# Cross attention: a batch's output projection in two parts of four pairs, with eight places for outputs and four for halves

## What is computed

```python
qh = (q @ wq.T).reshape(B, Sq, N_HEADS, HEAD_DIM).transpose(0, 2, 1, 3)
kh = (k @ wk.T).reshape(B, Sk, N_HEADS, HEAD_DIM).transpose(0, 2, 1, 3)
vh = (v @ wv.T).reshape(B, Sk, N_HEADS, HEAD_DIM).transpose(0, 2, 1, 3)
scores = jnp.einsum('bhqd,bhkd->bhqk', qh, kh) / jnp.sqrt(jnp.float32(HEAD_DIM))
attn = jax.nn.softmax(scores, axis=-1)
ctx = jnp.einsum('bhqk,bhkd->bhqd', attn, vh)
ctx = ctx.transpose(0, 2, 1, 3).reshape(B, Sq, N_HEADS * HEAD_DIM)
return ctx @ wo.T
```

## Time and profile before

| | us |
|---|---|
| median of 3 executions | 3653.69 |
| lowest and highest | 3648.0, 3655.38 |
| span of the profiled execution, first to last instruction | 3648.2 |
| cross attention, first row maximum to the last low half (rows below) | 1853.5 to 3440.3 |
| its 32 steps that open a batch, batches 1, 2, 3 | 205.2, 204.7, 206.4 |
| its 32 steps that close a batch, batches 0, 1, 2 | 197.1, 198.7, 197.3 |

### The profile page before, as it was taken

How to read it: one execution, slowest core, us unless ns; L and a number is a source line. 1 busy time by engine, 2 the same in 40 slices (tenths; PEclk the granted TensorE clock), 3 DMA queues, 4 the chain that set the end, 5 groups by cost and what they waited for, 6 DMA issues and landing times. The chain is left out here.

```text
span 3648.2 us, 78625 instructions
## 1 busy us (share of the span) xinstructions
PE 3088.9 (85%) x31124; PEld 1836.6 (50%) x31124; DVE 2698.1 (74%) x4017; ACT 2360.0 (65%) x4397; POOL 1058.4 (29%) x1854
## 2 busy tenths in 40 slices
PE   6999999978999755899778888998899879998824
PEld 3747474645665543444345554555455545555411
DVE  4748483867897765444469988889888988889688
ACT  3838373766786534333368887778777887788534
POOL 2232323156446234233212222222222222222122
PEclk9999999989999977999999999999999999999956
DMA  4050505175365376344399999999999999999843
GB/s 151 28 146 29 172 5 146 37 249 149 122 201 165 94 251 208 81 119 127 92 220 190 190 199 199 199 202 186 214 196 200 189 214 194 199 201 184 158 158 124
DMA packets 1309823, 582.40 MB, mean 160 GB/s; under 512 B 1144338, under 2 KB 1230994, under 8 KB 1306900
## 3 DMA queue, kind: packets, MB, share of 16 engines
q1 hardware_dynamic: 1305428, 560.60, 69.3%
q0 software_dynamic: 4032, 16.78, 1.2%
HBM read 183.63 MB, written 109.45 MB: 80 GB/s over the span
## 5 line engine op out<-in xcount | busy, mean ns | idle before, releaser
L2296 DVE SCALAR_TENSOR_TENSOR ca_halves<-ca_probs,ca_inv,ca_halves 128x1024 f16<-128x1024 f32 x512 | 655.5, 1280 | 109.9 <-ACT ca_halves L2222 102.4
L2288 DVE TENSOR_REDUCE ca_neg_max<-banks 128x1 f32<-128x1024 f32 x512 | 623.8, 1219 | 64.1 <-PE banks L2066 62.6
L2222 ACT ACTIVATE ca_halves<-ca_probs,ca_inv 128x1024 f16<-128x1024 f32 x512 | 586.6, 1146 | 102.9 <-DMA ca_pt<-ca_halves 99.1
L2214 ACT ACTIVATE ca_probs<-banks,ca_neg_max 128x1024 f32<-128x1024 f32 x512 | 568.7, 1111 | 72.6 <-DVE ca_neg_max L2288 70.7
L2032 POOL TENSOR_SCALAR ca_inv<-ca_total 128x1 f32<-128x1 f32 x512 | 97.5, 190 | 1197.1 <-ACT ca_probs L2214 1197.1
L2066 PE MATMUL banks<-ca_kt,ca_qt 64*128 64x512 f16 x3072 | 381.3, 382 | 48.8 <-ACT ca_probs L2214 47.1
L2088 PE MATMUL banks<-ca_pt,ca_v 128*64 128x256 f16 x6144 | 388.6, 277 | 0.9 <-DMA ca_pt<-ca_halves 0.8
L2088 PEld LDWEIGHTS banks<-ca_pt,ca_v 128*64 128x64 f16 x6144 | 318.6, 111 | 94.2 <-issue 78.4
L2035 POOL TENSOR_TENSOR ca_inv<-ca_inv,ca_minus_one 128x1 f32<-128x1 f32 x512 | 280.3, 548 | 42.6
L2066 PEld LDWEIGHTS banks<-ca_kt,ca_qt 64*128 64x128 f16 x3072 | 132.6, 95 | 238.8 <-issue 95.0
L2047 PE MATMUL banks<-ca_ct,ca_w 128*128 128x512 f16 x768 | 180.5, 386 | 48.1 <-DMA ca_ct<-ctx_part 23.8
(11 more groups left out here) (306 smaller groups left out, 5738.7 us busy)
## 6 DMA issues: line engine op xcount, KB each, us to landing
ca_w<-ca_w_parts SPq DMA_DIRECT2D x32, 768.0 KB, 5.4
wa_v<-v_rows SPq DMA_DIRECT2D x44, 264.0 KB, 4.5
v_rows<-wa_v_stage SPq DMA_DIRECT2D x32, 264.0 KB, 2.2
wa_x<-in_x SPq DMA_DIRECT2D x32, 256.0 KB, 5.3
wa_ring<-in_x SPq DMA_DIRECT2D x32, 256.0 KB, 3.9
x_after_window_attention<-wa_ring SPq DMA_DIRECT2D x32, 256.0 KB, 3.1
ba_tokens<-wa_tok_turned SPq DMA_DIRECT2D x32, 256.0 KB, 3.6
ba_xt<-ba_tokens SPq DMA_DIRECT2D x32, 256.0 KB, 7.2
```

The costliest lines, as they stand in the source:

```text
L2214: act.activation(probs[:, slot, :], scores(i), ACT.Exp, bias=neg_max[:, slot:slot + 1], accum_out=total[:, slot:slot + 1]).then_inc(exped, 1)
L2222: act.activation(halves[:, slot, 0, :], probs[:, slot, :], ACT.Copy, scale=inv[:, slot:slot + 1]).then_inc(split_hi, 1)
L2288: dve.tensor_reduce(out=neg_max[:, slot:slot + 1], in_=scores(i), axis=X_AXIS, op=ALU.max, negate=True).then_inc(maxed, 1)
L2296: dve.scalar_tensor_tensor(out=halves[:, slot, 1, :], in0=probs[:, slot, :], scalar=inv[:, slot:slot + 1], in1=halves[:, slot, 0, :], op0= ...
```

## The change

The output projection of batches 0, 1 and 2 is made in two parts, as it was in the last batch before. The first part is pairs 0 to 3, in steps 34, 37, 42, 45, 54, 55, 56 and 57 of the *same* batch; DVE adds each result to the residual rows. The second part is pairs 4 to 7, in the old places in the next batch. Each part has 12 matmuls for each tile where there were 24. The last batch keeps its six and two pairs. Steps that now hold a first part are no longer free for a flip, so 12 flips are left of 36, and 24 more units send both halves through the DMA transpose. `ca_ot` goes from 11 places to 8, and ACT waits for the part that last read a place (`released`). `ca_halves` goes from 3 places to 4, so `high_half` of unit i waits for the transpose of unit i-4; `ca_probs` and the score banks keep three.

```diff
-OT_SLOTS = PAIRS + 3
+OT_SLOTS = PAIRS
+HALF_SLOTS = 4
@@
-        halves = sb("ca_halves", [P, SLOTS, 2, S], F16)
+        halves = sb("ca_halves", [P, HALF_SLOTS, 2, S], F16)
@@
+        def first_step(b, t):
+            return BATCH * b + (34, 37, 42, 45, 54, 55, 56, 57)[t]
+
+        def tile_pairs(b):
+            return range(PAIRS // 2, PAIRS) if b + 1 < B else range(EARLY_PAIRS, PAIRS)
+
+        def early_step(b, t):
+            return first_step(b, t) if b + 1 < B else STEPS - 10 + t
+
+        def early_pairs(b):
+            return range(PAIRS // 2) if b + 1 < B else range(EARLY_PAIRS)
+
+        def released(turn, at):
+
+            b, pair = divmod(turn, PAIRS)
+            return 2 * NT * b + (NT if pair >= len(early_pairs(b)) else 0) + 2 * at + 2
@@
-        partly_at = {STEPS - 10 + t: t for t in range(NT)}
+        partly_at = {early_step(b, t): (b, t) for b in range(B) for t in range(NT)}
@@ SP
                             sp.dma_start_transpose(pt[:, step % 4, h, 0:parts * NT, :],
-                                                   halves[:, i % SLOTS, 0:parts, :].rearrange("p q s -> p (q s)")
-                                                   ).then_inc(turned[i % SLOTS], 16)
+                                                   halves[:, i % HALF_SLOTS, 0:parts, :].rearrange("p q s -> p (q s)")
+                                                   ).then_inc(turned[i % HALF_SLOTS], 16)
@@ PE
-                        out_product(b, t, range(PAIRS) if b + 1 < B else range(EARLY_PAIRS, PAIRS)).then_inc(out_projected, 1)
+                        out_product(b, t, tile_pairs(b)).then_inc(out_projected, 1)
                     if step in partly_at:
+                        b, t = partly_at[step]
                         spare_free(step)
                         pe.wait_ge(wo_loaded, 32)
-                        pe.wait_ge(ot_lo, GROUPS * (B - 1) + 4 * EARLY_PAIRS)
-                        out_product(B - 1, partly_at[step], range(EARLY_PAIRS)).then_inc(partly_projected, 1)
+                        pe.wait_ge(ot_lo, GROUPS * b + 4 * len(early_pairs(b)) - 4 + t // 2 + 1)
+                        out_product(b, t, early_pairs(b)).then_inc(out_projected, 1)
@@ ACT
-                    if i >= SLOTS:
-                        act.wait_ge(turned[slot], turned_by(i - SLOTS))
+                    if i >= HALF_SLOTS:
+                        act.wait_ge(turned[i % HALF_SLOTS], turned_by(i - HALF_SLOTS))
@@ ACT
-                        act.wait_ge(out_projected, NT * (last_use // PAIRS) + 2 * (g % 4) + 2)
+                        act.wait_ge(out_projected, released(last_use, g % 4))
```

More of the change, by code:

```diff
@@ L1903, in cross_attention @@
         split_hi, split_lo = sem("ca_split_hi"), sem("ca_split_lo")
-        turned = [sem(f"ca_turned{i}") for i in range(SLOTS)]
+        turned = [sem(f"ca_turned{i}") for i in range(HALF_SLOTS)]
         weighted, ot_hi, ot_lo = sem("ca_weighted"), sem("ca_ot_hi"), sem("ca_ot_lo")
         out_projected = sem("ca_out_projected")
-        partly_projected, partly_added = sem("ca_partly_projected"), sem("ca_partly_added")
+        partly_added = sem("ca_partly_added")
         qscale = 1.0 / (WS * DX ** 0.5)
@@ L1945, in turned_by @@
         def turned_by(i):
-            return 16 * (i // SLOTS + 1)
+            return 16 * (i // HALF_SLOTS + 1)
         def qk_item(turn, i, bank):
@@ L2077, in weigh @@
                             pe.wait_ge(ot_lo, g)
-                        for i in range(4 * g + 1, 4 * g + 4):
-                            pe.wait_ge(turned[i % SLOTS], turned_by(i))
+                        for i in range(4 * g, 4 * g + 4):
+                            pe.wait_ge(turned[i % HALF_SLOTS], turned_by(i))
                         if flips_until(4 * g + 3):
@@ L2122, in flip_low @@
                         last = pe.transpose(bank[:, kb * P:(kb + 1) * P],
-                                            halves[:, i % SLOTS, 1, kb * P:(kb + 1) * P], consts.ident_h[:, :])
+                                            halves[:, i % HALF_SLOTS, 1, kb * P:(kb + 1) * P], consts.ident_h[:, :])
                     last.then_inc(low_flipped, 1)
@@ L2219, in high_half @@
                     act.wait_ge(inverted, i + 1)
-                    if i >= SLOTS:
-                        act.wait_ge(turned[slot], turned_by(i - SLOTS))
-                    act.activation(halves[:, slot, 0, :], probs[:, slot, :], ACT.Copy,
+                    if i >= HALF_SLOTS:
+                        act.wait_ge(turned[i % HALF_SLOTS], turned_by(i - HALF_SLOTS))
+                    act.activation(halves[:, i % HALF_SLOTS, 0, :], probs[:, slot, :], ACT.Copy,
                                    scale=inv[:, slot:slot + 1]).then_inc(split_hi, 1)
@@ L2272, in low_item @@
                         rows = n.residual_rows(dve, b, t)
-                        dve.wait_ge(out_projected, NT * b + t + 1)
-                        if b + 1 == B:
-                            dve.wait_ge(partly_added, t + 1)
+                        dve.wait_ge(out_projected, 2 * NT * b + NT + t + 1)
+                        dve.wait_ge(partly_added, NT * b + t + 1)
                         dve.scalar_tensor_tensor(out=rows, in0=psum[:, SPARE, :], scalar=1 / WS, in1=rows,
@@ L2278, in low_item @@
                     if step in partly_at:
-                        t = partly_at[step]
-                        rows = n.residual_rows(dve, B - 1, t)
-                        dve.wait_ge(partly_projected, t + 1)
+                        b, t = partly_at[step]
+                        rows = n.residual_rows(dve, b, t)
+                        dve.wait_ge(out_projected, 2 * NT * b + t + 1)
                         dve.scalar_tensor_tensor(out=rows, in0=psum[:, SPARE, :], scalar=1 / WS, in1=rows,
@@ L2293, in low_half @@
                     dve.wait_ge(split_hi, i + 1)
-                    if i - SLOTS in flipped_units:
-                        dve.wait_ge(low_flipped, flips_until(i - SLOTS))
-                    dve.scalar_tensor_tensor(out=halves[:, slot, 1, :], in0=probs[:, slot, :],
-                                             scalar=inv[:, slot:slot + 1], in1=halves[:, slot, 0, :],
+                    if i - HALF_SLOTS in flipped_units:
+                        dve.wait_ge(low_flipped, flips_until(i - HALF_SLOTS))
+                    dve.scalar_tensor_tensor(out=halves[:, i % HALF_SLOTS, 1, :], in0=probs[:, slot, :],
+                                             scalar=inv[:, slot:slot + 1], in1=halves[:, i % HALF_SLOTS, 0, :],
                                              op0=ALU.mult, op1=ALU.subtract).then_inc(split_lo, 1)
```

## The result

The changed kernel takes 3632.95 us (median of 4, 3626.99 to 3635.51) beside 3654.53 us of the kernel before in the same comparison: a ratio of 0.9939, 95% interval 0.9926 to 0.9953. It is faster by 21.6 us. The prediction said 3588 us, range 3562 to 3628: the direction was right, the size a third of the forecast, and the time lies outside the range. The profiled execution took 3635.51 us.

A forecast was written before the change was run, and what follows sets the result against it. PE was taken to bind the opening halves of batches 1 to 3, nothing shown the closing ones. Terms -52 - 2 - 9 - 2 = -65 us took the 3648.2 us span to 3583, plus 5.5 gives 3588; range 3562 to 3628.

The forecast's parts named there:

- Tile turns: Opening halves of batches 1 to 3: twelve turns go from 616.3 us to 564, 47.0 each, -52 us.
- a tile step is now a step like the six of the yardstick: Opening halves: a tile step costs what six balanced full steps cost before, 5.82 us, so eight are 46.6 us.
- it is not above ... unless the queue binds: Upper bound of an opening turn: no longer than the present 51.4 us (gain 0) unless the transpose queue binds.
- I take -3 us a batch, near the byte count less one unit: Last ten steps of batches 0 to 2: -3 us each, -9 in all, bounds -9 to +6 a batch.
- The fourth place: Extra place for halves, in batch 0's opening half and the last batch's closing half: -2 us, between 0 and some -10.
- now stall PE: Last ten steps of a batch: flips that hold PE waiting for ACT's copy, 17.9 us in all, would be gone.
- The other closing turns: Closing halves of batches 0 to 2, two turns before the context loads: 47.1 us becomes 46.7, -2 us in all.
- Three places just suffice: Places for halves: a loop of some 7.4 us fits three units' 8.7 us, so waits are short; four give 11.6.
- Rival B: Places for halves were the stage's real loop, so more of the 99.1 us wait returns: 3566 us, chance 0.13.
- A: Rival: the transpose queue becomes the bound, turns stop at 49 us, opening halves give -28: 3626 us, chance 0.17.
- C: Rival: DMA engines carry no more than 203 GB/s, tile turns stay at 51 us, slower: 3694 us, chance 0.05.
- What was costed at nothing: SP's unchanged number and order of DMAs, and eight `ca_ot` places whose new wait on ACT finds its semaphore passed: 0 us.

## Why the prediction was wrong

**Tile turns.** The step "a tile step is now a step like the six of the yardstick" holds for every engine: 46.5 us is what turns 8, 16 and 24 take, and all twelve once bytes are taken away (46.5 to 46.9). It failed on "it is not above ... unless the queue binds": I put the queue's price under the engines'. I judged the queue by the 235 GB/s of the earlier trace rows and found 44.0 us for a turn's 10.35 MB. That row is a mix in which 2.6 of 6.8 MB are plain loads; a whole transpose moves its 0.52 MB in 2.52 us, 208 GB/s. The price by itself was 47.8 us, above the engines' 46.5, and the measured turns behind each batch's first averaged 49.6. The term was -52 and is -30.5; the price accounts for 10 of the 22 us that are missing, the rest is the remainder named above.

**Batch ends.** The step "I take -3 us a batch, near the byte count less one unit" is the one with the wrong sign: +1.8, +4.5 and +2.0. Its own byte count, by the same 235 GB/s, said nothing gained, and I took the fourth place's 2.9 us off it three times. The fourth place was right: alone it gives 2.6, 3.0 and 3.9 us there. The whole transposes were not nothing: they cost 6.0 to 6.6 us a batch end, over the 4.4 of the price. Each flip had been saving 1.11 us of DMA time by that price. That the flips that "now stall PE" were a symptom of late transposes is my reading, which no run tests.

**The other closing turns** were to be 46.7; they are 46.4 where nothing is behind, but 50.1, 47.8 and 50.6, 46.5 in turns 12, 13, 20, 21. A backlog of the opening half that drains there would do that; but the kernel without the weights, whose opening turns are not late, has 47.4 and 47.2 us in turns 12 and 20, so it is not all.

**The fourth place.** I gave it -2 us apart from the rest; it measured -31 us alone. "Three places just suffice" was worked out with the median landing, 4.8 us. The likely reason is the late ones of 6 to 8 us, the longest of which stood behind the context loads; no run varies the landing alone. In the 47.1 us of a flip turn I saw a step's price and not a wait; of the 4.3 us of DVE's idle in it a fourth place gives 1.9 back. Rival B had this mechanism, with a chance of 0.13. But B's 3566 us needed the path to carry 46.5 us turns too.

**The rivals.** A came nearest: the turn stopped at 49 us and the total within 7 of its 3626. That the total is so near is in part luck: A had -28 for the opening halves and nothing else, the stage had -30.5, +10.7 in the closing halves, and -5.6 in its first and last half. My sum of 41 us against A used the median issue of 2.17 us, which mixes whole transposes with half ones; a whole one alone is 2.40 us. What A called the queue's bound is what the path carries; whether SP's issue or the DMA engines set it stays open. With the other DMAs moved off SP nothing was gained, which speaks for the engines, but other waits came in their place. By the rule of the Trainium skill's "Perfetto Trace Analysis" ("What 'DMA-bound' means") that I weighed, a solid track of DMA slices on the issuing sequencer means that this sequencer binds. The trace does not let the rule decide: the slices are solid here, but 434 us of the stage's 1561 are SP's waits. The rule's outcome, that a lighter PE gives nothing, did not come in the opening halves (-30.5 us). The Trainium skill's page "DMA: Bandwidth & Descriptors", section "Latency and other measured facts", gives 261 GB/s for a DMA transpose with a non-contiguous middle dimension on one kernel; this one ran at 208 GB/s by itself. C's mechanism, a rate near what a tile turn showed, was right in kind, and its 203 GB/s was nearer than my 235 to the 208 and 214 of the run of DMAs alone; it was wrong in that before's tile turns were not at the rate but at PE's 51 us, so the move had 3 us to give.

**What was costed at nothing** cost nothing: the new wait for `released` shows in no list of waits, the part's read-out of 0.68 us is under the step, and DVE's 177.6 us a half are hidden.

Left open: what sets the price of the path, SP's issue or the DMA engines; the 1 us a turn above it; why batch ends differ from one batch to the next by up to 4 us at the same work (62.6, 66.4 and 63.6 us with half transposes); and how much of the 31 us of the fourth place is in each turn's weights.

## What to carry to other kernels

Price a queue in the time of its own kind of transfer, not in GB/s of a mixed stretch, and add up what a balanced turn asks of it *before* crediting an engine's relief: here the path needed 47.8 us a turn where the engines needed 46.5. When an engine is relieved by giving up something that unloads a second resource, count the second. And try the extra buffer alone first: it was a small edit, and the rest of the change, which moved 2.65 us off each of 24 tiles, was worth nothing beside it.

## What the runs showed of the hardware

Back to back, a DMA transpose from SBUF to SBUF of 128 x 2048 fp16 took 2.52 us and landed 4.7 us after its issue began; one of half the size took 1.41 us, more than half. SP's issue of one lasted 2.40 us in the median with nothing else to do, nearly the whole of its share of the path. The very first, on an idle queue, already took 2.18 us, so this run does not show that the DMA engines hold the issue back. Other traffic does lengthen it: in the changed kernel the first one behind a turn's weights took 4.21 us with its data ready (last row), and 16 of them with 1.8 MB of plain traffic took 47.8 us.

```profile
L72 SPq DMA_TRANSPOSE pt<-halves x48: 2172/2404/2847, 17.4 to 133.9; - x48
L87 SPq DMA_TRANSPOSE pt<-halves x48: 1232/1336/1349, 381.4 to 446.1; - x48
17.38 2.18 SPq L72 DMA_TRANSPOSE pt<-halves  x1
2371.03 4.21 SPq L2026 DMA_TRANSPOSE ca_pt<-ca_halves  x1
```
